# A two-layer gated attention block on one core: the last layer's eight experts computed for the chosen rows only, in tiles of 256 rows

## The reference, cut to what matters

```
x = x + tanh(g_xattn[1]) * xattn1(ctx, layernorm(x), ...)      # its output is layer-normed with g_o, b_o
x = x + tanh(g_ffn[1]) * ffn1(layernorm(x), Wg, W1, W2, W3)
# ffn1: E = 8 experts, K = 2 chosen, D = 128, H = 256
gate_out = einsum('bsd,ed->bse', x, Wg)
top_v, top_i = top_k(gate_out, 2); probs = softmax(top_v)
for e in range(E):
    w_e = sum(probs * (top_i == e))
    h1, h2 = x @ W1[e].T, x @ W2[e].T
    out += (silu(h1) * h2) @ W3[e].T * w_e
```

## Time and profile before

| | us |
|---|---|
| median of 3 runs (range) | 1411.18 (1409.85 to 1411.53) |
| profiled execution, its own time | 1409.91 |
| its span, first to last instruction | 1407.9 |
| busy: PE, DVE, ACT, POOL | 1186.7, 1085.4, 931.6, 903.1 |

### The profile page before, as it was taken

One profiled execution on the slowest core, in us unless ns is written; L12 is line 12 of the kernel. 1 busy time (PEld: TensorE's weight loads), 2 busy tenths in 40 slices (PEclk: granted clock), 3 DMA queues, 4 the chain that ended last, 5 costly groups with the idle time before them and its releaser, 6 DMA issues. The chain is left out here.

```text
span 1407.9 us, 39161 instructions
## 1 busy us (share of the span) xinstructions
PE 1186.7 (84%) x14613; PEld 889.4 (63%) x14613; DVE 1085.4 (77%) x2846; ACT 931.6 (66%) x1858; POOL 903.1 (64%) x855
## 2 busy tenths in 40 slices
PE   1578999949874699999999999999994688888887
PEld 1445777734542488888887878787873355555555
DVE  5888888867868666767767676868675799998996
ACT  0668999936655488787887878787872455454554
POOL 0250999945767366676666666666663477777778
PEclk9669555559995799999999999999997799999999
DMA  9100000001220011111111211112111000000000
GB/s 228 55 1 1 13 16 16 16 10 27 42 53 1 1 32 32 32 32 32 25 32 32 32 25 32 32 32 30 31 29 23 1 2 9 8 7 7 7 8 16
DMA packets 121437, 37.30 MB, mean 26 GB/s; under 512 B 105876, under 2 KB 119612, under 8 KB 121276
## 3 DMA queue, kind: packets, MB, share of 16 engines
q1 hardware_dynamic: 110235, 31.70, 10.8%
q10 hardware_dynamic: 11040, 3.42, 1.0%
HBM read 9.92 MB, written 2.10 MB: 9 GB/s over the span
## 5 line engine op out<-in xcount | busy, mean ns | idle before, releaser
L1178 POOL TENSOR_TENSOR attention_pl_l<-attention_probs_l,attention_ph_l 128x512 f16<-128x512 f32 x128 | 148.4, 1159 | 180.3 <-ACT attention_ph_l L1348 180.3
L1412 DVE TENSOR_REDUCE attention_negmax<-bank 128x2 f16<-128x410 f32 x256 | 137.7, 579 | 136.3 <-PE bank L1257 136.0
L1594 POOL TENSOR_TENSOR mixture_hidden_l<-mixture_hidden,mixture_hidden_h 128x512 f16<-128x512 f32 x128 | 148.4, 1160 | 74.8 <-ACT mixture_hidden_h L1681 74.8
L612 POOL TENSOR_TENSOR attention_probs_l<-attention_probs,attention_probs_h 77x512 f16<-77x512 f32 x128 | 145.5, 1153 | 52.7 <-ACT attention_probs_h L694 48.5
L1178 POOL TENSOR_TENSOR attention_pl_c<-attention_probs_c,attention_ph_c 77x512 f16<-77x512 f32 x128 | 147.8, 1155 | 0.0
L1690 ACT ACTIVATE mixture_tanh<-bank 128x512 f32<-128x512 f32 x128 | 76.4, 597 | 105.3 <-PE bank L1641 105.3
L1639 PE MATMUL bank<-mixture_xs,moeh 128*128 128x512 f16 x256 | 98.2, 383 | 32.0 <-DVE mixture_hidden L1772 32.0
L1272 PEld LDWEIGHTS bank<-identh,attention_negmax 128*128 128x128 f16 (+1 forms) x1024 | 83.3, 107 | 55.7
L1240 PE MATMUL bank<-layer_kv,ah 128*128 128x128 f16 x1024 | 108.7, 220 | 11.1 <-PEq L89 11.0
L1348 ACT ACTIVATE attention_probs_l<-bank 128x512 f32<-128x512 f32 x128 | 76.4, 597 | 56.8 <-PE bank L1272 56.8
L1268 PE MATMUL bank<-attention_th,layer_kv 128*128 128x512 f16 (+1 forms) x256 | 97.0, 379 | 14.7 <-issue 14.5
(11 more groups left out here) (323 smaller groups left out, 4788.0 us busy)
## 6 DMA issues: line engine op xcount, KB each, us to landing
X<-in_x SPq DMA_DIRECT2D x4, 512.0 KB, 9.2
out<-X SPq DMA_DIRECT2D x8, 256.0 KB, 2.3
attention_turned_h<-attention_heads_h SPq DMA_TRANSPOSE x96, 2.3
attention_turned_l<-attention_heads_l SPq DMA_TRANSPOSE x96, 2.3
ctx<-in_ctx SPq DMA_DIRECT2D x1, 1232.0 KB
setup_nat_w<-in_w SPq DMA_DIRECT2D x1, 1024.0 KB, 14.6
setup_nat_f<-in_fw ACTq DMA_DIRECT2D x2, 256.0 KB, 6.9
setup_nat_q<-in_q ACTq DMA_DIRECT2D x1, 512.0 KB, 8.3
```

What stands on the lines that cost most here:

```text
L612: pool.tensor_tensor(probs_l[:, n % SLOTS], probs[:, n % 2], probs_h[:, n % SLOTS], ALU.subtract).then_inc(p_split, 1)
L1178: last = pool.tensor_tensor(low[:, g % 2], whole[:, g % 2], high[:, g % 2], ALU.subtract)
L1412: last = dve.tensor_reduce(negmax[:, g, 2 * i:2 * i + 2], score[i], AX.X, ALU.max, negate=True)
L1594: pool.tensor_tensor(hidden_l[:, e % 4, j], hidden[:, e % 2, j], hidden_h[:, e % 4, j], ALU.subtract).then_inc(hid_lo, 1)
```

## The change

The mixture is computed by routing. While `attention1` runs, and in 14 further turns of its body behind the last sequence (`ROUTED = 14`), each batch k of four sequences passes through these steps, placed a fixed number of sequences behind the batch's start: norm factors on POOL (`row_scale`, 16 operations each time, for the attention's output and for the new rows), applied on ACT; rows split into high and low fp16 (`pay_high`, `fill`) and turned by four DMAs; gates (`choose`), `top_two` and `which`; `select`, `number` (a row's rank within its expert, by matmuls with a triangle of ones), `find`, `multiply`, `places`; then eight indirect DMAs from POOL (`send`), each writing 128 rows of 544 bytes to their places in a DRAM table, where every expert has a region. `guess`, `newton` and `out_norm` of DVE go. At the end DVE makes a table of at most 39 tiles of 256 rows (which expert, which first row). The third `split_transposed` and `mixture` go. `experts` loops over the 39 tiles, written out: SP turns a tile from DRAM into SBUF, TensorE multiplies by the tile's expert (its weights are found by a register that is read from the table), ACT and DVE as before (DVE now makes the low part too), ACT copies the result out, POOL scatters 256 rows to DRAM by two indirect DMAs. Behind the last tile the 4 MB of results are read back, DVE multiplies by the shares and adds to X, ACT stores.

`setup` fills the DRAM table (34560 rows of 544 bytes) with a blank row by one DMA on SP, and two more clears of semaphores with barriers are added. The core of the diff:

```diff
+T = 256
+ROW = 2 * 128 + 16
+TILES = (2 * B * S + E * (T - 1)) // T
+ROWS = E * B * S + (TILES - 2 * B * S // T) * T
@@ setup, SP, behind its waits for the loads
+            sp.wait_ge(blank_in, 1)
+            sp.dma_start(w.tokens.rearrange("(t p) r -> p t r", p=128),
+                         w.blank[:].unsqueeze(1).broadcast_to([128, ROWS // 128, ROW])).then_inc(w.cleared, 16)
@@ attention1, POOL
+            def row_scale(i, var, mean, eps):
+                y, z = rstd[:, i], shift[:, i]
+                link(pool.tensor_scalar(part[:], var, eps, None, ALU.add))
+                link(pool.tensor_scalar(y.bitcast(INT32), part[:].bitcast(INT32), -0.5, float(0x5F3759DF), ALU.mult, ALU.add))
+                for _ in range(3):
+                    link(pool.tensor_tensor(z, y, y, ALU.mult))
+                    link(pool.tensor_tensor(z, z, part[:], ALU.mult))
+                    link(pool.tensor_scalar(z, z, -0.5, 1.5, ALU.mult, ALU.add))
+                    link(pool.tensor_tensor(y, y, z, ALU.mult))
+                link(pool.tensor_scalar(z, mean, -1.0, None, ALU.mult))
+                return pool.tensor_tensor(z, z, y, ALU.mult)
+            def x_scale(k):
+                pool.wait_ge(xchain, k + 1)
+                row_scale(1, w.mv[:, batch(k), 1], w.mv[:, batch(k), 0], EPS).then_inc(x_scaled, 1)
...
+            def body(b):            # behind probs_low and heads_low of each g
+                    k = ending(b, 6)      # out_scale at g == 0, gain and residual at g == 2
+                    k = ending(b, 7)      # x_scale at g == 2
+                    k = ending(b, 8)      # fill at g == 2
+                    k = ending(b, 9)      # differ at g == 2, select at g == 3
+                    k = ending(b, 11)     # multiply at g == 0, count_up at g == 1
+                    for q in range(2 * BATCH):
+                        k = ending(b - (2 + q) // G, 11)
+                        if k is not None and g == (2 + q) % G:
+                            send(k, q)
@@ attention1, TensorE: project(t) now waits for two DVE reads of the same bank
+                k = ending(t, 7)
+                if k is not None:
+                    pe.wait_ge(topped, 2 * k + 1)
+                k = ending(t, 9)
+                if k is not None:
+                    pe.wait_ge(rank_read, k + 1)
@@ attention1, DVE, at the end of the unit's program
+                    k = ending(b, 7)      # statistics_x at g == 1, aggregate_x at g == 2
+                    k = ending(b, 9)      # top_two at g == 1, which at g == 2
@@ experts
+            for n in range(TILES):                                            # SP
+                row = sp.value_load(w.table[0:1, 0, n:n + 1], min_val=0, max_val=ROWS - T)
+                if n >= RX:
+                    sp.wait_ge(h_done, n - RX + 1)
+                sp.dma_start_transpose(xt[:, n % RX], w.tokens[bass.ds(row, T), 0:2 * D]).then_inc(x_in[n % RX], 16)
...
+            for n in range(TILES + LAG):                                      # TensorE
+                if n < TILES:
+                    rise(n, pe.value_load(w.table[0:1, 1, n:n + 1], min_val=0, max_val=MH * (E - 1)))
+                if n >= LAG:
+                    fall(n - LAG, pe.value_load(w.table[0:1, 1, n - LAG:n - LAG + 1], min_val=0, max_val=MH * (E - 1)))
...
+            for n in range(TILES + LAG + 1):                                  # ACT
+                if n < TILES:
+                    squash(n)             # tanh, 128 x 512
+                if 1 <= n < TILES + 1:
+                    hidden_high(n - 1)    # copy, 128 x 512
+                if n < TILES:
+                    number(n)             # register load, DMA of 256 row numbers of 4 bytes
+                if n >= LAG + 1:
+                    copy_out(n - LAG - 1) # copy, 128 x 256
...
+            def send(n):                                                      # POOL
+                pool.wait_ge(y_copied, n + 1)
+                pool.wait_ge(id_in[n % RI], 16 * (n // RI + 1))
+                for r in range(T // S):
+                    pool.indirect_dma_start(w.outputs, bass.IndirectOffsetOnAxis(ap=ids[:, n % RI, r].bitcast(UINT32), axis=0),
+                                            y_rows[:, n % RY, r], None, bounds_check=2 * B * S - 1,
+                                            oob_is_err=False).then_inc(y_out[n % RY], 16)
@@ flamingo: the third split_transposed and mixture are replaced by
+        nc.clear_and_free_semaphores(w.spent)
+        nc.all_engine_barrier()
+        experts(nc, a, w, bank)
```

More of the change, by code:

```diff
@@ L1236, in _, with body @@
+            def body(t):
+                if t < B:
+                    if t >= 2:
+                        sp.wait_ge(projected, t - 1)
+                    for half in range(2):
+                        heads(t, half)
+                k = ending(t, 7)
+                if k is not None:
+                    rows(k)
+            sequences(body)
         @block.tensor
@@ L1329, in _ @@
             sequences(body)
[L1330 to L1333 removed]
+            pe.wait_ge(counted_up, BATCHES)
+            pe.matmul(count, w.ones_h[:], so_far[:], start=True, stop=True).then_inc(counted, 1)
         @block.scalar
@@ L1375, in copy_out, with out_norm @@
                 act.activation(out[:, t % (2 * BATCH)], out_p, ACT.Copy).then_inc(out_copied, 1)
-            def body(b, u, first, last):
+            def out_norm(k):
+                act.wait_ge(out_scaled, k + 1)
+                if k:
+                    act.wait_ge(summed, k)
+                for t in range(BATCH * k, BATCH * k + BATCH):
+                    i = t % BATCH
+                    last = act.activation(zn[:, i], out[:, t % (2 * BATCH)], ACT.Identity, bias=shift[:, 0, i:i + 1],
+                                          scale=rstd[:, 0, i:i + 1])
+                last.then_inc(out_normed, 1)
@@ new lines, in aggregate_x, with top_two, which @@
+                last.then_inc(xchain, 1)
+            def top_two(k):
+                dve.wait_ge(gated, k + 1)
+                if k:
+                    dve.wait_ge(diffed, k)
+                dve.tensor_copy(gate[:].rearrange("p c e -> p (c e)"), gates).then_inc(topped, 1)
+                dve.wait_ge(topped, 2 * k + 1)
+                for c in range(BATCH):
+                    last = dve.max(top[:, c], gate[:, c])
+                last.then_inc(topped, 1)
+            def which(k):
+                dve.wait_ge(topped, 2 * k + 2)
+                if k:
+                    dve.wait_ge(selected, k)
+                for c in range(BATCH):
+                    last = dve.max_index(index[:, c], top[:, c], gate[:, c])
+                last.then_inc(indexed, 1)
@@ L1815, in flamingo @@
+            for n in range(TILES):
+                send(n)
 def flamingo(nc, a):
```

829 lines of the change are left out of this document (454 added, 375 removed).

## The result

The changed kernel took 1388.7 us (median of four runs, 1385.9 to 1389.4), the kernel before 1410.5 beside it: ratio 0.9846 (0.9834 to 0.9858), 21.8 us faster. I had forecast 1336, 75 us faster. The sign is right and the time stands in the wide range, 1290 to 1412, but outside my own narrower one, 1305 to 1370. The size is wrong by 53 us: 22 us gained in place of 75.

What follows compares the result with a forecast made beforehand. Second attention and mixture were read as bound by TensorE. Span 1407.9 + 0 (setup) + 54 (second attention) - 129 (tail and experts) = 1333, so 1336 us measured; own range 1305 to 1370, wide range 1290 to 1412.

Steps and rivals of the forecast that it cites:

- 1. Setup: Setup's new fill of 34560 pieces: SP's issue 12 us, within 17 us free, data landing in 77 us; cost 0.
- Rival A: In the setup SP is held by the fill, all engines stand up to 60 us: +55, 1391 us; chance 0.2.
- 2. Second attention: Routing work put into the second attention, four costs against each unit's slack behind TensorE: together +54 us.
- the wait for `top_two`: Second attention: `project` waits for DVE's copy, TensorE standing still 2.4 us in each of 7 batches: 17 us.
- 22 + 10: Second attention, POOL's costs: 22 us for `x_scale`'s linked steps and 10 us for the sends.
- its additions: Second attention: TensorE's 16 gate matmuls, at most 0.7 us a batch: 5 us.
- 3. Tail: Routing's last batch behind the attention, nothing hidden: experts start 52.5 us after DVE has the last statistics.
- Barriers and clears: In the tail of routing, before the experts: 2 us, an estimate with no row.
- 4. Experts: 39 tiles at ACT's 2.9 us, 113 us; with tail, landing, read-back and clock 203.5 against 332.6 before: -129.
- rival D: Experts' tiles run at TensorE's pace, register loads hidden: 2.2 to 2.3 us each, -25, 1311 us; chance 0.15.
- Rival B: Attention, tail and tiles: a send costs POOL much more than its own operations; at 2.5 us, 1481; chance 0.15.
- Rival C: TensorE's clock stays low in the experts: a tile takes 4.2 us, +51, 1387 us; chance 0.1.

Runs made afterwards that it cites:

- late_project: Changed kernel with TensorE's projection and ACT's copy of it one unit later in the second attention: 1332.3 us.
- short_scale: Changed kernel with one Newton round in place of three in POOL's `x_scale` (8 of its 16 linked steps left out): 1359.8 us.
- attn_plain: Changed kernel with the second attention's 64 row scatters from POOL replaced by plain DMAs from SP, rows stored in order: 1325.6 us.
- first trace: Trace of the changed kernel behind the 1388.7 us result, with many late TensorE signals: span 1384.1 us.
- first condition: Runs in which 24 or more TensorE signals in the second attention were late; the unedited changed kernel took 1388.7 and 1390.0 us.
- second trace: Trace of the unedited changed kernel from the group of runs at 1349.8 us, with few late TensorE signals: span 1347.2 us.
- after_third: The changed kernel unedited, run a third time, with 31 late TensorE signals in the second attention: 1390.0 us.
- after_again: The changed kernel unedited, run again beside the kernel before, with 4 late TensorE signals: 1349.8 us, ratio to before 0.9581.
- fixed_expert: Changed kernel with expert 0's weights for all tiles, so no register load or register address on TensorE: 1333.1 us, again 1332.8.
- x_scale_dve: Changed kernel with `x_scale`, the 16-step scale of the router's rows, moved from POOL back to DVE: 1364.4 us.

## Why the prediction was wrong, by its steps

**1. Setup: right.** SP's issue took 0.41 us, less than the 12 I had allowed, and the fill landed in 71 us (77 forecast). The first mixing matmuls of the second attention began at 485.3, where before they did at 484.3. TensorE's first matmul behind the setup came at 61.2 us (59.8 before). Rival A is refuted; the 5 us that its sum takes off for a queue's depth (60 less 55) were an estimate that no run shows.

**2. Second attention: the sum right, +54 forecast, in part by luck.** From the first mixing matmul to the last it is 582.1 us before and 629.5 after, +47.4. From there to DVE's last statistics it is 8.1 us more (17.0 for 8.9), since TensorE's last projection stands behind the gate matmuls of the batch before, and they wait for the DMA turns of its rows:
```profile
1127.23 0.59 PE L1487 MATMUL bank<-wgt,attention_rows_t 128*128 128x8 f16 x16 [9.62 <-DMA attention_rows_t<-attention_pay]
1128.20 0.27 PE L1475 MATMUL bank<-o1h,attention_turned_h 128*128 128x128 f16 x1 [0.38 <-DVE attention_gate L1720]
```
That is time I had not placed. Together with the setup's 1.0 it is +56.5. The terms: the wait for `top_two` was 13.2 in 6 waits (17 in 7), POOL 32.0 (22 + 10), of which 7.1 is one wait in the last unit, where TensorE has nothing else. (The 10 for sends was itself too high: 40.4 of work less 36.6 and 2.4 of slack is 1.4 a batch, 7 in all, and not 1.9.) Against these 45.2 us waits that the kernel before had are gone, so that standing still grew by 31.8 only. TensorE's busy time grew by 15.6, where I had 5 for its additions and nothing for the clock. So 47.4 for 54 comes from two misses in opposite directions, and the 9.1 us at the two ends bring it to 56.5. `late_project` and `short_scale` show that the waits for `top_two` and for POOL are both on the path. A linked step costs 0.28 us (0.27), and a send is on POOL 0.98 us, 1.29 from start to start (1.3). "DVE loses 3.5 us a batch of its own norm work, which gives nothing back" was wrong by 1.2 us: at units 8 and 9 of a batch that much came back (-0.4 and -0.8), and that is part of what is gone.

**3. Tail: 52.5 forecast, 58.6.** The scales took 4.5 us each (4.3), and the eight last sends 1.27 apart (1.3). The miss is "Barriers and clears 2, an estimate with no row": POOL's drain behind its last send alone took 5.29 us (1178.82 to 1184.11). In `attn_plain`, with no send ahead of it, it took 0.03, so it belongs to the price of the sends.

**4. Experts: the step that failed.** "ACT is the longest: 2.9, and 39 x 2.9 = 113 us" takes the fullest engine of a loop as its pace. It went wrong twice.
- Where signals are prompt TensorE is longer than ACT, as rival D had it, but not at D's price, because it too has register loads, and I counted them only for ACT (0.5 us, an estimate with no row; 0.28 in the first trace). I had 2.2 to 2.3 for TensorE. Without loads a tile takes 2.54 us (99.1 / 39), with two 3.11 (121.2 / 39). That error is 4 us of the sum, small because ACT's 2.9 was near by chance. Nor was DVE's low part 0.29 us: it took 683 ns.
- In the first condition a tile takes 3.92 us (152.8 / 39): 31.6 us more for the stage by the same instructions. The cause shown is the send: in a group whose second attention has 32 late signals, take the sends of the results away and the rises' signals are prompt and the stretch is 122.5; pace them and it is 130.2. Rival B had a send cost POOL more than its operations. POOL's price was as forecast; what it costs is TensorE's signals. No row of the trace before has a send, so no row could show it, but the prediction has no place at all for a cost that one engine's operation puts on another's semaphores.

The rest of the stage: 20.3 us (13 forecast) to `combine`, 17.5 in the second trace. Most of this miss has nothing to do with late signals: when the last `rise` ends four tiles are still to be sent, eight sends 1.29 us apart (1311.6 to 1320.7 in the second trace), and with plain stores it is 12.0. I had 9 us from the last `rise` to the landed results, with no row for it. `combine` is right, 20.6 for 21.1.

Sum in the first trace: +2.5, +6.1, +35.8, +7.3, -0.5 = +51.2. In the second: +1.4, +4.7, +4.2, +4.5, -0.5 = +14.3, the forecast within 1.1%. Rival C is not it: the clock was 0.91 over the tiles' stretch. It was low for the first 4.4 us and then seven times for 3.4 us (matmuls of 256 columns 0.21 us apart in place of 0.11), behind TensorE's long stops; it follows from the waiting. (C's 1.9 and 3.84 us for 4608 columns are what the trace of before gives: there, matmuls of 512 columns followed each other every 0.216 us at clock 1.00 and every 0.427 us at 0.50 in the median, so nine of them take 1.94 and 3.84 us.) Of the 31.6 us it can be little by the profile: TensorE's busy time in the tiles is 102.0 us for 98.5.

**Open.** What puts a run in one condition or the other. It was constant within each group of runs. Of the last two groups, which ran on a chip of the same number, one had late signals and the other had not, so the chip alone does not decide. Nor is it shown by which path a send holds TensorE's signals, or why it holds some and not others.

## What to carry to other kernels

Price a new kind of operation by what it does to the others' semaphores (here 31.6 us over the tiles), not only by its own engine's time: where an engine waits and the view names no releaser, compare the end of the producer's work with the start of its consumer. In a loop over four engines the fullest engine is only a lower bound (2.9 us a tile by that here, and 3.92 and 3.11 in the two traces); look for what is done in pairs. Here a wait of 3.4 us or more on TensorE cost more than its length, since the granted clock was 0.50 for at least 3.4 us behind it: compare the busy time too. A kernel whose time differs between groups of runs needs the kernel it is compared with in the same group.

## What the runs showed of the hardware

- While POOL issues an indirect DMA (0.98 us), signals of TensorE's matmuls can be held until 1.2 to 1.9 us behind its start (14 of the 25 that were due 0.30 to 0.98 us into one); with four in a row they came up to 2.95 us (3.2 in `after_third`) behind the end of their matmul. ACT's and DVE's came 0.01 us behind the end of their work. Traces of the same program showed it in two groups of runs and not in two others.
- A register load on TensorE took 0.30 to 0.32 us in the median (at most 0.48) and 0.15 for the work on the register behind it (both traces); two loads a tile and the addresses made from them cost 0.57 us of TensorE's pace (stretch 121.2 for 99.1, `after_again` and `fixed_expert`).
- POOL's drain at the end of the second attention took 5.29 us where it stood behind sends (18 traces) and 0.03 where there were none (`attn_plain`).
- Behind each wait of 3.4 to 3.9 us in the second attention TensorE's granted clock was 0.50 for 3.4 us of full work (first trace). With waits of 1.2 to 1.6 us in those places (`short_scale`) it stayed at 1.00.
- A DVE operation on 128x4 with two operands took 1.06 and 2.19 us in place of 0.16 where it began during an operation of POOL with two operands, and ended with one (`x_scale_dve`).
- An issue of 34560 pieces into an empty queue took 0.41 us, about as much as one of 512 (0.38 to 0.44).
